# Cross-attention and a routed FFN on one core: key blocks, a norm and a guard change engines

## The reference

```python
q, k, v = heads(ln(x) @ Wq + bq), heads(ln(x) @ Wk + bk), heads(ln(x) @ Wv + bv)   # 16 heads of 8
y  = softmax(causal(q k^T / sqrt(8))) v
y += softmax(qc kc^T / sqrt(8)) vc           # qc from ln(x), kc and vc from 64 context rows
x1 = x + y @ Wp + bp
h  = ln(x1)
aff = sigmoid(h @ Wr + br)                   # 32 experts
w   = top8(aff) / (sum(top8(aff)) + 1e-9)
out = x1 + shared_expert(h) + sum_e w[e] * expert_e(h)      # silu(h Wg) * (h Wu), then Wd
```

## Time and profile before

| what | value |
|---|---|
| median of three runs | 205.09 us (204.45 to 206.31) |
| the profiled execution, whole time | 207.16 us |
| its span, first to last instruction | 205.4 us |
| TensorE busy | 190.5 us, 93% |
| VectorE busy | 160.7 us, 78% |
| ScalarE busy | 135.7 us, 66% |
| GpSimd busy | 97.9 us, 48% |
| mean granted TensorE clock | 0.981 |

### The profile page before, as it was taken

The page is one execution under the profiler, slowest core; times in us unless marked ns, Lnnn a source line. Parts: engine busy times, 40 slices in busy tenths (PEclk is TensorE's granted clock), DMA queues, the critical chain, the costliest instruction groups (busy, mean ns, idle before and its releaser), DMA issues.

```text
span 205.4 us, 3982 instructions
## 1 busy us (share of the span) xinstructions
PE 190.5 (93%) x1237; PEld 140.4 (68%) x1249; DVE 160.7 (78%) x375; ACT 135.7 (66%) x272; POOL 97.9 (48%) x154
## 2 busy tenths in 40 slices
PE   7969899999999999788999899699899999999993
PEld 2537667777777777666675776488688887887662
DVE  2888997788689977996594889748957879877982
ACT  3544898787898889886779453645545655555571
POOL 6899972343463757339455386665522231100020
PEclk9996999999999999999999999979999999999998
DMA  4365333233342334201201112210000000000003
GB/s 114 94 137 145 100 78 84 50 73 83 71 121 67 77 86 102 54 0 42 65 15 38 38 40 54 51 32 0 3 0 3 0 0 2 0 0 3 0 0 102
DMA packets 20434, 10.40 MB, mean 51 GB/s; under 512 B 11881, under 2 KB 18542, under 8 KB 20414
## 3 DMA queue, kind: packets, MB, share of 16 engines
q1 hardware_dynamic: 19290, 9.24, 18.2%
q0 software_dynamic: 672, 0.69, 1.5%
q10 hardware_dynamic: 452, 0.23, 0.5%
HBM read 4.51 MB, written 0.52 MB: 25 GB/s over the span
## 4 chain that ended last, share of the span: by engine, by line
PE 69%; DVE 11%; issue 8%; ACT 5%; POOL 4%; DMA 1%; DVEq 0%; POOLq 0%; ACTq 0%
PE psum L1358 10%; PE psum L1360 9%; PE psum L1359 9%; PE psum L1461 6%; PE psum L1517 5%; PE psum L1542 4%; PE psum L1554 4%; POOL hid_lo L707 3%; PE psum L1522 3%; PE psum L1564 3%; PE psum L1460 2%; PE psum L1689 2%; PE psum L1526 2%; PE psum L1503 2%; PE psum L1483 2%
## 5 line engine op out<-in xcount | busy, mean ns | idle before, releaser
L925 ACT ACTIVATE gate<-psum,bias_cols 128x512 f32<-128x512 f32 (+2 forms) x35 | 23.5, 675 | 31.5 <-PE psum L1360 31.5
L802 ACT ACTIVATE probs<-psum 128x512 f32<-128x512 f32 x64 | 36.3, 596 | 1.9 <-PE psum L1522 0.8
L707 POOL TENSOR_TENSOR hid_lo<-hid,hid_hi 128x512 fp32r<-128x512 f32 x13 | 16.7, 1287 | 32.7 <-ACT hid_hi L934 30.5
L1302 DVE SCALAR_TENSOR_TENSOR gated<-psum,bias_cols,gate 128x512 f32<-128x512 f32 x32 | 24.0, 749 | 10.5 <-ACT gate L925 7.9
L934 ACT CAST hid_hi<-hid 128x512 fp32r<-128x512 f32 (+1 forms) x33 | 20.2, 613 | 6.3 <-DVE hid L1314 4.5
L1461 PE MATMUL psum<-key_blocks,query_rows 96*128 96x512 f32 x48 | 24.1, 544 | 0.0
L1314 DVE TENSOR_TENSOR hid<-gated,psum 128x512 f32<-128x512 f32 x32 | 21.9, 683 | 2.8 <-PE psum L1689 1.1
L638 POOL TENSOR_TENSOR w_late_lo<-w_ffn,w_late_hi 128x384 fp32r<-128x384 f32 x11 | 12.3, 1116 | 20.0 <-ACT w_late_hi L814 20.0
L663 POOL TENSOR_SCALAR_AFFINE_SELECT probs<-probs 128x512 f32<-128x512 f32 x16 | 10.1, 634 | 20.7 <-ACT probs L802 20.6
L1092 DVE TENSOR_REDUCE row_max<-psum 128x4 fp32r<-128x1024 f32 x16 | 19.4, 1214 | 0.0
L1088 DVE TENSOR_REDUCE row_max<-psum 128x4 fp32r<-128x512 f32 x16 | 11.0, 689 | 8.6 <-PE psum L1461 8.5
(11 more groups left out here) (198 smaller groups left out, 515.1 us busy)
## 6 DMA issues: line engine op xcount, KB each, us to landing
query_rows<-queries SPq DMA_DIRECT2D x46, 64.0 KB, 2.0
key_rows<-keys SPq DMA_DIRECT2D x39, 32.0 KB, 1.9
w_ffn<-in_L_ffn_Wg SPq DMA_DIRECT2D x16, 64.0 KB, 2.0
w_ffn<-in_L_ffn_Wu SPq DMA_DIRECT2D x16, 64.0 KB, 2.1
w_ffn<-in_L_ffn_Wd SPq DMA_DIRECT2D x16, 64.0 KB, 2.1
ckey_rows<-ckeys POOLq DMA_DIRECT2D x12, 32.0 KB, 2.0
key_rows<-keys POOLq DMA_DIRECT2D x9, 32.0 KB, 2.0
x_sb<-in_x SPq DMA_DIRECT2D x2, 128.0 KB, 2.9
```

Source lines behind the costliest of these rows:

```text
L707: pool.tensor_tensor(hid_lo[:, n % 3, :], hid[:, n % 3, :], hid_hi[:, n % 3, :].bitcast(F32), ALU.subtract).then_inc(pool_lo_done, 1)
L802: act.activation(probs[:, i % 2, c, :], bank(B_ST + c % 2), ACT.Exp, scale=SCALE).then_inc(exp_done, 1)
L925: act.activation(gate[rows_of(n), n % 3, part], psum[of, B_GATE + n % 2, part], ACT.Silu, bias=bias_cols[of, BIAS_GATE + u:BIAS_GATE + u + ...
L1302: dve.scalar_tensor_tensor(out=gated[:, n % 3, :], in0=bank(B_UP + n % 2), scalar=bias_cols[:, BIAS_UP + u:BIAS_UP + u + 1], in1=gate[:, n ...
```

## The change

1. **Key blocks.** From step 5 on, the two blocks of `expand` that VectorE made (`tensor_scalar`) are made by GpSimd (`tensor_tensor` with the mask broadcast). That is 11 pairs, 22 instructions. GpSimd's `expand(i+3)` stands at the head of its step `i`, ahead of that step's causal selects. TensorE and SyncE wait for a new semaphore there.
2. **Batch 3's second norm.** VectorE's two instructions at `(4, "C")` become two ScalarE activations at `(5, "A")`, between the gate of item 5 and `hid_hi` of item 4. They need minus mean times rstd, which GpSimd makes with two more small operations (`last_norm`); it no longer waits for the norm itself.
3. **The guard.** TINY is added by ScalarE just before its silu, and VectorE's reciprocal moves from the `router` piece to the `top` piece, one item later.
4. **1e-9.** `top` has a ninth column that holds 1e-9, so the sum over it needs no separate addition (L1205 goes, four times).
5. **Idle products.** 12 instead of 8 ahead of `natural(0)`, and 3 more after `turn_max(0)`.

```diff
+        def first_blocks(i):
+            if i < POOL_BLOCKS:
+                return v_blocks_set, 2 * i + 2
+            return pool_blocks_set, 2 * (i - POOL_BLOCKS) + 2
...
+            def expand(i):
+                pool.wait_ge(*keys_of(*divmod(i, GROUPS)))
+                pool.wait_ge(m_st, 4 * (i - RING) + 4)
+                for j in (0, 1):
+                    blocks, rows, mine = key_block(i, j)
+                    pool.tensor_tensor(blocks, rows, mine.to_broadcast([ROWS, SEQ]),
+                                       ALU.mult).then_inc(pool_blocks_set, 1)
             for i in range(STEPS):
+                if POOL_BLOCKS <= i + 3 < STEPS:
+                    expand(i + 3)
                 pool.wait_ge(exp_done, 4 * i + 2)
...
+            def last_norm():
+                mine = slice(TILES - 2, TILES)
+                pool.wait_ge(var2_ready, BATCH)
+                chain(pool.tensor_tensor(rstd[:, mine], var_eps[:, mine], minus_half[:, 0:2], ALU.pow))
+                chain(pool.tensor_tensor(minus_mean[:, :], moments[:, mine, 0], rstd[:, mine], ALU.mult))
+                pool.tensor_tensor(neg_mean[:, mine], zeros[:, :], minus_mean[:, :], ALU.subtract).then_inc(have_rstd, 1)
             for n in POOL_LO[:-1]:
                 if n == RSTD_ITEM:
-                    tail("project", BATCH - 1)
+                    last_norm()
...
                     if name == "router":
+                        act.wait_ge(logits_ready, b + 1)
+                        act.activation(logits[:, :, :], logits[:, :, :], ACT.Identity,
+                                       bias=tiny[:, 0:1]).then_inc(logits_guarded, 1)
                         act.wait_ge(logits_guarded, b - 1)
                         act.activation(exp_neg[:, :, :], logits[:, :, :], ACT.Silu).then_inc(silu_ready, 1)
+                    elif name == "norm":
+                        act.wait_ge(have_rstd, len(NORM_GROUPS) + b + 1)
+                        for t in range(2):
+                            k = 2 * b + t
+                            act.activation(x2_norm[:, t, :], x1[:, k, :], ACT.Identity, scale=rstd[:, k:k + 1],
+                                           bias=neg_mean[:, k:k + 1]).then_inc(x2_normed, 1)
...
-                    dve.tensor_scalar(logits[:, :, :], logits[:, :, :], TINY, None, ALU.add).then_inc(logits_guarded, 1)
-                    dve.wait_ge(logits_guarded, b - 1)
-                    chain(dve.reciprocal(r_logits[:, :, :], logits[:, :, :]))
...
                 if name == "top":
                     dve.wait_ge(silu_ready, b - 1)
+                    chain(dve.reciprocal(r_logits[:, :, :], logits[:, :, :]))
...
-                    chain(dve.tensor_scalar(top_sum[:, :], top_sum[:, :], 1e-9, None, ALU.add))
...
-                if i + 3 < STEPS:
+                if i + 3 < POOL_BLOCKS:
                     expand(i + 3)
...
-            run_idle(8, B_CK)
+            run_idle(12, B_CK)
...
             turn_max(0)
+            run_idle(3, B_MISC)
```

More of the change, by code:

```diff
@@ L31 @@
 RING = 4
+POOL_BLOCKS = 5
 EXPERTS, TOP, INNER = 32, 8, 64
@@ L95, in build @@
         minus_half = sb("minus_half", [P, TILES])
+        minus_mean = sb("minus_mean", [P, 2])
+        zeros = sb("zeros", [P, 2])
+        tiny = sb("tiny", [P, 1])
         head_mask = sb("head_mask", [P, GROUP])
@@ L146, in build @@
         silu_table = sb("silu_table", [P, 2])
-        top = sb("top", [P, 2, TOP])
+        top = sb("top", [P, 2, TOP + 1])
         not_top = sb("not_top", [P, 2, EXPERTS])
@@ L202, in build @@
         pool_ckey_blocks_set = sem("pool_ckey_blocks_set")
+        pool_blocks_set = sem("pool_blocks_set")
         ckey_rows_set = sem("ckey_rows_set")
@@ L345, in build @@
                       (3, "A"): [("y_turn", 3)],
+                      (5, "A"): [("norm", 3)],
                       (6, "C"): [("route_turn", 2), ("x2_turn", 3)],
@@ L354, in build @@
                     (4, "A"): [("weights", 2)],
-                    (4, "C"): [("norm", 3)],
                     (7, "A"): [("x2_turn", 3)],
@@ L466, in place_batch @@
                     i = 4 * (b - 2) + g
-                    sp.wait_ge(v_blocks_set, 2 * i + 2)
+                    sp.wait_ge(*first_blocks(i))
                     sp.wait_ge(a_blocks_set, 2 * i + 2)
@@ L563, in _ @@
             pool.memset(key_rows[:, :, :, :].bitcast(F32), -1.0).then_inc(rows_set, 1)
+            pool.memset(zeros[:, :], 0.0)
+            pool.memset(tiny[:, :], TINY)
             pool.memset(bias_rows[:, :], 0.0).then_inc(bias_rows_set, 1)
@@ L676, in _ @@
                     chain(pool.memset(route[:, :, :, :], 0.0))
+                    pool.memset(top[:, :, TOP:TOP + 1], 1e-9)
                     pool.memset(route[:, :, :, 2 * EXPERTS:2 * EXPERTS + 1], 1.0).then_inc(zeroed, 1)
@@ L1165, in tail_rest @@
                     norm_stats(x1, mine, var2_ready)
-                if name == "router" and b >= 2:
-                    dve.wait_ge(logits_ready, b + 1)
-                    dve.tensor_scalar(logits[:, :, :], logits[:, :, :], TINY, None, ALU.add).then_inc(logits_guarded, 1)
-                    dve.wait_ge(logits_guarded, b - 1)
-                    chain(dve.reciprocal(r_logits[:, :, :], logits[:, :, :]))
                 if name == "router" and b < 2:
@@ L1183, in best_of @@
                 for t in range(2):
-                    ins = dve.max(top[:, t, :], affinity[:, t, :])
+                    ins = dve.max(top[:, t, 0:TOP], affinity[:, t, :])
                 chain(ins)
                 for t in range(2):
-                    dve.match_replace(not_top[:, t, :], top[:, t, :], affinity[:, t, :], -1.0)
+                    dve.match_replace(not_top[:, t, :], top[:, t, 0:TOP], affinity[:, t, :], -1.0)
             def long_part(name, b):
@@ L1201, in long_part @@
                 if name == "weights":
+                    if b == 0:
+                        dve.wait_ge(zeroed, 4)
                     chain(dve.tensor_reduce(top_sum[:, :], top[:, :, :], AX.X, ALU.add))
@@ L1210, in long_part @@
                         dve.wait_ge(t_route, b - 1)
-                    if b == 0:
-                        dve.wait_ge(zeroed, 4)
                     to = route[:, b % 2, :, :]
@@ L1451, in natural @@
                     pe.wait_ge(have_idents, 1)
-                pe.wait_ge(v_blocks_set, 2 * i + 2)
+                pe.wait_ge(*first_blocks(i))
                 pe.wait_ge(a_blocks_set, 2 * i + 2)
```

## The result

The changed kernel takes 204.59 us (median of 20 runs) beside 205.86 us of the kernel before (20 runs). The ratio is 0.993, with a 95% interval of 0.9903 to 0.9958: 0.7% faster. The forecast was 203.4 us by a shift of -1.7; the shift of the medians is -1.3. So 204.59 is 1.2 above the forecast: 0.8 because with more runs before's median is 205.86 and not 205.09, and 0.4 by the shift. It lies just above the forecast's own range (202.4 to 204.5) and inside the range for 8 in 10. The profiled execution took 203.28 us with a span of 201.5, so the two profiled spans differ by 3.9 us, three times as much as the medians. That difference is the first thing to explain.

A forecast was written before the change was run, and what follows sets the result against it. TensorE, 93% busy, was taken as the bound, other engines counting only where it waits for them. -1.6 + 0.35 + 0.2 - 1.2 + 0 + 0.55 = -1.7 from 205.09 gave 203.4 us; own range 202.4 to 204.5, 8 in 10 201.2 to 205.7.

The forecast's parts named there:

- Step 1: Attention steps 11 and 12: key blocks and L1205 off VectorE shorten TensorE's stalls, gain 1.6 us (1.2 to 2.4).
- Step 2: Same blocks on GpSimd, 1.24 us a pair: losses of 0.35 us at `natural(11)` and 0.2 at `natural(15)`.
- Step 3: Head: more idle products keep TensorE's clock at 2.4 GHz, gain 1.2 us (loss of 0.6 to gain of 1.5).
- Step 4: FFN item 4, ahead of `down(4)`: the second norm's move to ScalarE nets 0, within -0.3 and +0.5 us.
- Step 5: FFN, wait before `down(10)`: batch 3's guard and moved reciprocal lose 0.55 us, between 0 and 0.9.
- exclusion rival: At `natural(11)` and `natural(15)`: GpSimd and VectorE shut each other out, 2.7 us a pair, 206.3 us; chance 0.10.
- The second dip: Rival: the FFN's clock dip near 130 to 135 us goes too, 1.7 us more, 201.7 us; chance 0.25.

The follow-up runs named there:

- E2: The kernel before with only the changed kernel's idle products in the head (12 and 3): 204.55 us, ratio 0.9935 to before.
- E3: The changed kernel with all key blocks back on VectorE: 204.29 us.
- E4: The changed kernel with the guard and the reciprocal back on VectorE, ahead of `top`: 203.67 us.
- E1: The changed kernel with the head's idle products as before (8, and none before step 0's scores): 204.37 us, ratio 0.991 to before.
- E6: The kernel before with the changed kernel's on-chip tiles alone, instructions unchanged: 205.40 us.
- E8: The changed kernel with batch 3's second norm back on VectorE, after item 4's hid: 204.13 us.
- E11: E10 with batch 2's weights moved behind `hid(4)` and four idle products instead of six ahead of `down(4)`: 202.19 us, ratio 0.982 to before.
- E10: The changed kernel with the edits of E4, E5 and E7 together: 202.08 us, ratio 0.981 to before.
- E12: E11 with ScalarE's second norm of batch 3 behind `hid_hi(4)` and no idle products in the FFN: 200.43 us, ratio 0.9752 to before.
- E7: The changed kernel with GpSimd spreading only the key blocks of steps 14 and 15, VectorE the rest: 202.94 us.
- E9: The kernel before with idle products in both places, 12 and 3 in the head and six ahead of item 4's down: 204.72 us, ratio 0.994.
- E5: The changed kernel with six more idle products ahead of `down(4)`: 202.93 us, ratio 0.9843 to before.

## Why the prediction was right, and where it wasn't

The direction, the size within 0.4 us and the places of steps 1 to 3 hold. That the size fits is in part luck. E2 has before's work behind the changed kernel's head, and neither its trace nor the changed kernel's has a stretch, so between these two only the work counts. From the first `attend_self` to the end TensorE takes 168.08 us in E2 and 166.61 in the changed kernel, 1.47 less:

| place | forecast | E2 to changed |
|---|---|---|
| attention (steps 1 and 2) | -1.05 | -1.11 |
| FFN's start to `down(4)` (step 4) | 0 | +0.17 |
| `down(4)` to `down(18)` (step 5) | +0.55 | +0.30 |
| behind `down(18)` | 0 | -0.83 |

The forecast for these was -0.5. Step 3's -1.2, of which the medians show little, stood in for the 0.83 that I had not foreseen.

- **Step 1** (-1.6). Stalls left are 0.30 and 0.77 for 0.28 and 0.5. The pairs give 0.90 net of the two losses (E3), so about 1.46 gross, and the column's 0.20 comes on top, as a shorter step and not as a shorter wait. I had it shorten the second wait, which is why 0.77 stands there and not 0.5. Right in sum.
- **Step 2** (+0.35, +0.2). Measured 0.31 and 0.25; the pair 1.24 (2 × 621 ns) for 1.24. The exclusion rival's 2.7 us a pair appears nowhere: the mean of 621 ns leaves no room for it. The rule behind it is real but hits other instructions, those of E4.
- **Step 3** (-1.2). The mechanism is right where the clock falls: 0.99 between the traces of E1 and the changed kernel. What failed is the move from the trace to the median. The profiled execution of before, 207.16, had both stretches; 15 of 29 had one or none. I subtracted a gain that only executions with the head's stretch have from a median in which all are mixed. I also argued that 1.2 us gaps in steps 11 and 12 don't lower the clock; E6 shows an execution in which it falls there.
- **Step 4** (0). 0.15 at `down(4)` (E8), within the bounds. It was a tie: `hid(4)` and the norm end within 0.4 us of each other. The weights' move alone gains nothing (E11), the norm's return to VectorE 0.15 (E8), and both moves together, against E10, 1.6 us (E12).
- **Step 5** (+0.55). Size right, 0.50 (E4), or less where `route` fares better: the wait is 0.16 in E8, 0.17 in E7, and E3 has none. Place wrong: it is a wait at `route_turn(3)` and not a longer one at `down(10)`. The yT wait of item 3 is not this edit's: E9 has it too (0.24).
- **The second dip** as a rival was put wrongly. It isn't either there or gone: one stretch is left in 10 of 19 executions and two in 2, and E5 shows that they keep the median 1.3 us above the profiled execution.
- **Not in the sum at all:** the 0.8 us after 165 us. Some 0.3 to 0.5 are the tiles' places (E6). Another 0.4 is a collision in before's item 18, gone in the changed kernel. E2, E6 and E9 have it too. The timeline of before, VectorE, GpSimd and TensorE:

```profile
168.52 0.75 DVE L1302 SCALAR_TENSOR_TENSOR gated<-psum,bias_cols,gate 128x512 f32<-128x512 f32 x1 [0.73 <-ACT gate L925]
169.19 1.41 DVE L974 TENSOR_TENSOR hid_lo<-hid,hid_hi 128x512 fp32r<-128x512 f32 x1
...
169.04 1.01 POOL L638 TENSOR_TENSOR w_late_lo<-w_ffn,w_late_hi 128x384 fp32r<-128x384 f32 x1 [3.29 <-ACT w_late_hi L814]
...
170.66 0.50 PE L1358 MATMUL psum<-hid_hi,w_late_hi 128*128 128x512 f32 x1
```

`gated` starts 0.36 us later than in the items around it, so GpSimd is first and VectorE's `hid_lo`, shut out meanwhile, takes 1.41 us instead of 0.68; TensorE takes 2.57 and 2.44 us for two items of 2.32. The changed kernel has the same delay at 179.05, where GpSimd has nothing to do, and loses nothing. What delays `gated` is open. Seven traces have such a delay, each with a packet of an instruction queue (q14) 0.65 to 0.93 us behind the start of the late `gated`. In the other seven the packet passes too, 1.0 us or more behind the last `gated`, and no `gated` near it is late. No run tests whether it is the cause.

Both medians of the result, 205.86 and 204.59, lie where the groups with one stretch lie (205.87 and 204.65). So their -1.3 is mainly work, which is worth 1.2 to 1.7 us (the groups with one stretch, those without, 204.78 to 203.30, and E9 to E5), and 0.8 of that was not foreseen. That executions with two stretches have become rarer (14 of 29 in the table, then 2 of 19) moves these two medians little. Whether the head's idle products pay in the changed kernel stays open: no profile with them has a stretch in the head, but E6's, without them, has none there either, and E1's median is no higher.

## What to carry to other kernels

Before you sum over a profile, look at the times and clocks of many executions: a profile is one draw, and a gain that lies in a stretch at 1.2 GHz counts only in the share of executions that have it. A few idle products in the one long wait of TensorE can be worth as much as all the moves of work around it (204.59 to 202.93 in E5), and shortening that wait is better still (200.43 in E12). When an instruction is moved and nothing happens, look for a second one that is due at the same moment, and move both.

## What was not expected of the hardware

- The granted clock of the same program on the same input differs between executions: 204.8, 205.9 or 207.3 us in before, with a mean clock near 1.00, 0.99 or 0.98. In the profiles that is 0, 1 or 2 stretches at 1.2 GHz, at three places, each behind a wait of TensorE of 1.2 to 1.7 us.
- The places of tiles on the chip change the pitch of products in a dense stretch, 232 against 227 ns, with the same instructions.
- When VectorE and GpSimd operate on tiles at the same time, starts 0.01 us apart or less decide whether a 0.22 us operation takes 1.09 us, and a delay of 0.36 us can cost TensorE 0.4 or nothing, by what GpSimd does then.
